# One order of start-up work for another in a fused tokenizer, attention and expert kernel: the gate's tanh, the token projection, the norm of pair 1 and the first maxima are moved

## The reference, cut to what matters

```python
def dwconv(x, wd, wp, bp):            # 3x3 depthwise, then 1x1
    return conv(conv(x, wd, pad=((1, 1), (1, 1)), groups=x.shape[1]), wp, bp)
loc  = dwconv(gelu(conv(x, pl_w, pl_b, stride=16)), pl_dw, pl_pw, pl_pwb)
g    = gelu(conv(wavelet_packet(x), pg_w1, pg_b1))
glob = conv(gelu(dwconv(g, pg_dw, pg_pw, pg_pwb)), pg_w2, pg_b2)
gate = 0.5 * (jnp.tanh(alpha) + 1.0)
h = (1.0 - gate) * loc + gate * glob
h = relu(dwconv(h, f1_...)); h = relu(dwconv(h, f2_...))
t = tokens(dwconv(loc + h, f3_...))
t = (t - mean(t)) / sqrt(var(t) + 1e-05) * ln_g + ln_b
h = concat([cls, t, txt], axis=1)
h = h + attn(layernorm(h))            # 12 heads of 16, own key masked
h = h + ffn(layernorm(h))             # z-scored logits, softmax, then the best 2 of 4 experts
```

## Time and profile before

| | before |
|---|---|
| median of 3 runs | 1234.02 us (1228.44 to 1234.77) |
| the profiled execution | 1228.34 us, its span 1226.7 us |
| TensorE busy | 1097.7 us, 89% of the span |
| VectorE busy | 679.3 us, 55% |
| ScalarE busy | 394.5 us, 32% |
| mean granted TensorE clock | 0.947 |
| chain that ended last | TensorE 63%, VectorE 16%, ScalarE 4% of the span |

### The profile page before, as it was taken

One profiled execution on the slowest core, in us unless ns is written; L12 is line 12 of the kernel. 1 busy time (PEld: TensorE's weight loads), 2 busy tenths in 40 slices (PEclk: granted clock), 3 DMA queues, 4 the chain that ended last, 5 costly groups with the idle time before them and its releaser, 6 DMA issues.

```text
span 1226.7 us, 19327 instructions
## 1 busy us (share of the span) xinstructions
PE 1097.7 (89%) x7731; PEld 809.0 (66%) x7731; DVE 679.3 (55%) x1890; ACT 394.5 (32%) x901; POOL 45.5 (4%) x81
## 2 busy tenths in 40 slices
PE   4898797888799999899989998999899989888895
PEld 3443464555486678568857875777588657676795
DVE  1378666564744666557654765476547643623432
ACT  1222132223324333443334333432343234223221
POOL 4200000100000000000000000000000000000000
PEclk8999899999989899989999998999899999788998
DMA  9100061422052014203320332042204220040000
GB/s 262 50 1 0 20 176 29 74 60 38 16 116 46 9 40 101 46 9 59 82 46 9 71 69 45 10 87 53 46 9 87 53 46 2 10 87 2 2 9 9
DMA packets 39441, 60.80 MB, mean 50 GB/s; under 512 B 6660, under 2 KB 31224, under 8 KB 38776
## 3 DMA queue, kind: packets, MB, share of 16 engines
q1 hardware_dynamic: 36256, 56.84, 21.5%
q10 hardware_dynamic: 3096, 2.74, 0.9%
HBM read 42.77 MB, written 16.34 MB: 48 GB/s over the span
## 4 chain that ended last, share of the span: by engine, by line
PE 63%; DVE 16%; ACT 4%; issue 2%; DMA 1%; SPq 1%; POOL 0%; DVEq 0%; POOLq 0%
PE PS L696 15%; PE PS L674 12%; DVE mx L1368 7%; PE PS L795 6%; PE PS L889 5%; PE PS L830 5%; PE PS L803 4%; PE PS L836 3%; PE PS L898 2%; PE PS L845 1%; DMA qst<-mrows 1%; PE PS L927 1%; PE PS L770 1%; PE PS L1019 1%; DVE acc L724 1%
## 5 line engine op out<-in xcount | busy, mean ns | idle before, releaser
L696 PE MATMUL PS<-w,hid 128*128 128x192 f32 x1152 | 231.1, 339 | 2.5 <-DVE acc L724 1.9
L709 ACT ACTIVATE hid<-PS,b 128x370 f32<-128x370 f32 x192 | 109.2, 569 | 316.7 <-PE PS L674 315.1
L696 PEld LDWEIGHTS PS<-w,hid 128*128 128x128 f32 x1152 | 197.8, 197 | 13.2 <-issue 5.1
L1368 DVE TENSOR_REDUCE mx<-PS 128x2 f32<-128x356 f32 x288 | 127.4, 519 | 131.7 <-PE PS L830 99.0
L1107 ACT ACTIVATE probs<-PS 128x356 f32<-128x356 f32 x288 | 110.9, 486 | 22.3 <-PE PS L830 12.8
L674 PE MATMUL PS<-x2T_hi,w_hi 128*128 128x370 f32 x192 | 91.9, 479 | 0.0
L845 PE MATMUL PS<-masks,ident_bf 128*128 128x256 bf16 (+1 forms) x288 | 73.4, 256 | 0.0
L889 PE MATMUL PS<-probs,va 128*17 128x178 f32 x1536 | 67.3, 315 | 6.4 <-ACT probs L1107 6.4
L795 PE MATMUL PS<-xT,w_at 96*96 96x370 f32 x192 | 68.2, 500 | 2.6 <-ACT xT L1067 1.7
L830 PE MATMUL PS<-kst,qst 96*128 96x178 bf16 x384 | 64.7, 264 | 6.3 <-issue 2.2
L770 PE MATMUL PS<-masks,ident_bf 128*128 128x356 bf16 x351 | 62.4, 327 | 4.0 <-POOL hid L1693 4.0
(11 more groups left out here) (232 smaller groups left out, 1727.3 us busy)
## 6 DMA issues: line engine op xcount, KB each, us to landing
qst<-scr_q SPq DMA_DIRECT2D x96, 144.0 KB, 4.6
scr_q<-qs SPq DMA_DIRECT2D x16, 432.0 KB, 3.3
scr_k<-ks SPq DMA_DIRECT2D x16, 432.0 KB, 4.1
kst<-scr_k SPq DMA_DIRECT2D x16, 432.0 KB, 5.0
kst<-scr_k SPq DMA_DIRECT2D x16, 288.0 KB, 5.9
cols<-in_x_cols SPq DMA_DIRECT2D x6, 392.0 KB, 12.7
w<-in_w SPq DMA_DIRECT2D x1, 2304.0 KB, 29.4
kst<-scr_k SPq DMA_DIRECT2D x16, 144.0 KB, 6.3
```

The costliest lines, as they stand in the source:

```text
L696: ins = nc.tensor.matmul(tile_psum((6, 7), i), hid[u % 2][:, 128 * i:128 * i + 128], w2[:, u, :], start=(j == 0 and i != 1), stop=(j == FT ...
L709: nc.scalar.activation(hid[u % 2][:, 0:XN], PS[:, 4 + u % 2, 0:XN], ACT.Relu, bias=b1[:, u:u + 1]).then_inc(S["h_ready"], 1)
L1368: nc.vector.tensor_reduce(out, PS[:, g, 0:T2].rearrange("p (b j) -> p b j", b=2), AX.X, ALU.max)\
```

## The change

Ten edits, all ahead of the end of round one.

1. ScalarE copies the wavelet product into `cw` first and does the gate's tanh after it. The load of `rows` goes from ScalarE's queue to SyncE's, and a load `w_f3` of 147 KB is new.
2. In the first block TensorE has unread products at three more places: 7 ahead of the first 1x1 product, 5 and 9 ahead of those of step 2, 12 ahead of the last depthwise step.
3. The token projection is cut: images 0 to 6 in the first block, 7 to 15 at the start of the second. Its operands `flat`, `w_f3`, `mid` and `f3_bias` now lie in the space of `probs`, so that they live on.
4. The bias sum goes to the second block: first pair 0's tokens alone, the rest after the norm of pair 0's input.
5. `preset` is GpSimd's alone and is awaited at 1. VectorE's clearing goes behind the norm of pair 0's input and has a semaphore of its own, `cleared`, that the first maxima wait for.
6. The unread products in `pe_first` write bank 2 up to pair 1's turn; 44 become 40 and 85 become 70.
7. `tok_norm(dve, 1, PAIRS)` becomes `tok_norm(dve, 1, 2)`; the norm of pairs 2 to 7 goes into round one, behind the split of s = 1's query. GpSimd waits for it before it copies pair 2.
8. In round one the maxima of s = 0 are made in six units in PSUM banks 4 to 6, set between the steps of s = 1's front; they stood behind it.
9. `WARM` has fewer products in that front (31 become 16) and 4 for 15 behind it.
10. In round one `x2T_lo` is made between the query's split and the key's.

```diff
-    "norm": 4, "query": 9, "key": 6, "value": 0, "kc": 4, "g": 3, "u": 5, "ss": 4,
-    ("max", 0): (0, 0, 0, 0, 0, 0), ("split", 0): 15, ("rows", 0): 22, ...
+    "norm": 0, "query": 4, "key": 3, "value": 0, "kc": 3, "g": 2, "u": 4, "ss": 4,
+    ("max", 0): (0, 0, 0, 0, 0, 0), ("split", 0): 4, ("rows", 0): 22, ...
...
+        def tokens_of(lo, hi):
+            for i in range(lo, hi):
+                q, b = divmod(i, 2)
+                for k in range(2):
+                    ins = nc.tensor.matmul(PS[64 * b:64 * b + 64, 4 + q // 2, D * (q % 2):D * (q % 2) + D],
+                                           flat[:, k, NI * i:NI * i + 64], w_f3[:, k, :],
+                                           start=(k == 0), stop=(k == 1), skip_group_check=True)
+            ins.then_inc(f3_psum, 1)
...
-                    act.wait_ge(ld_const, 32)
-                    nc.scalar.activation(gate[:], chan[0:HC, C_ALPHA:C_ALPHA + 2], ACT.Tanh).then_inc(gate_ready, 1)
-
                     act.wait_ge(haar_psum, 1)
...
                     ins.then_inc(haar_ready, 1)
+
+                    act.wait_ge(ld_const, 32)
+                    nc.scalar.activation(gate[:], chan[0:HC, C_ALPHA:C_ALPHA + 2], ACT.Tanh).then_inc(gate_ready, 1)
...
+                    def warm(n):
+                        for _ in range(n):
+                            nc.tensor.matmul(PS[:, 7, 0:T2], ident_bf[:], masks[:], start=True, stop=True)
                     def depthwise(r, n, lo=PE_TAP0, hi=9):
+                        if r == 4 and n == 1:
+                            warm(12)
...
                         if r == 0:
                             pe.wait_ge(apart_ready, 2)
+                            pe.wait_ge(casts, 1)
+                            warm(0 if n else 7)
+                        if r == 2:
+                            warm(9 if n else 5)
...
+                    pe.wait_ge(flat_ready, 1)
+                    tokens_of(0, B // 2 - 1)
...
         def pe_first(pe):
-            pe_warm(44)
+            pe.wait_ge(flat_ready, 2)
+            tokens_of(B // 2 - 1, B)
+            pe_warm(40, 2)
             pe_turn_in(pe, 0, 0)
...
-            pe_warm(85)
+            pe_warm(70, 2)
...
+            pe.wait_ge(S["cleared"], 1)
...
         def dve_first(dve):
+            dve.wait_ge(f3_psum, 1)
+            nc.vector.tensor_tensor(img_tok[:, 0, :], ps[:, 0, 0], f3_bias[:, 0, :], ALU.add).then_inc(S["tok_sum"], 1)
+            dve.wait_ge(S["tok_sum"], 1)
             tok_norm(dve, 0, 1)
             splits = dve_front0(dve, 0)
+            nc.vector.memset(PS[:, 3, :], 0.0)
...
+            dve.wait_ge(f3_psum, 2)
...
             dve_value(dve, 0, 0)
-            tok_norm(dve, 1, PAIRS)
+            dve.wait_ge(S["tok_sum"], 2)
+            tok_norm(dve, 1, 2)
...
+                def unit(u):
+                    if beside:
+                        pe_max_unit(pe, 0, a, u, 4)
                 pe_turn_in(pe, 1, b)
+                if beside:
+                    pe_stacked(pe, 0, a)
+                    pe.wait_ge(S["v_ready", 0], at(a, 1, 1))
+                unit(0)
...
                 pe_query(pe, 1, b)
+                unit(1)
...
                 pe_key(pe, 1, b)
+                unit(2)
...
             last.finish()
+            for u in units[0:3]:
+                dve_max_unit(dve, 0, a, u, 4)
...
+            if m is None and a is not None:
+                tok_norm(dve, 2, PAIRS)
...
-                splits(b)
+                splits(b, low if m is None else None)
```

More of the change, by code:

```diff
@@ L114 @@
 WARM = {
-    "norm": 4, "query": 9, "key": 6, "value": 0, "kc": 4, "g": 3, "u": 5, "ss": 4,
-    ("max", 0): (0, 0, 0, 0, 0, 0), ("split", 0): 15, ("rows", 0): 22, ("exp", 0): (0, 0, 0, 0, 0, 0), ("out", 0): 0,
+    "norm": 0, "query": 4, "key": 3, "value": 0, "kc": 3, "g": 2, "u": 4, "ss": 4,
+    ("max", 0): (0, 0, 0, 0, 0, 0), ("split", 0): 4, ("rows", 0): 22, ("exp", 0): (0, 0, 0, 0, 0, 0), ("out", 0): 0,
     ("max", 1): (2, 2, 2, 2, 2, 0), ("split", 1): 15, ("turn", 0): 6, ("back", 0): 4, ("rows", 1): 4,
@@ L819, in pe_value, with pe_logits @@
             pe_tokens(front(s, r), 4 * s + 2, xT[s], S["v_psum", s])
-        def pe_logits(pe, s, r, u, rows_, still, move, read, filled):
+        def pe_logits(pe, s, r, u, rows_, still, move, read, filled, first=0):
             for bank in range(3):
@@ L918, in pe_deviation @@
             ins.then_inc(S["kc_psum"], 1)
+            unit(3)
             moe.point("kc")
@@ L928, in pe_deviation @@
             ins.then_inc(S["g_psum"], 1)
+            unit(4)
             moe.point("g")
@@ L935, in pe_deviation @@
             ins.then_inc(S["u_psum"], 1)
+            unit(5)
             moe.point("u")
@@ L1264, in dve_front0, with splits @@
             dve_scaled(0, h_in(r), xn[0]).then_inc(S["xn_ready", 0], 1)
-            def splits(before):
+            def splits(before, between=None):
                 dve.wait_ge(S["q_f32", 0], at(r, 1, 1))
@@ L1271, in splits @@
                 dve.wait_ge(S["q_split", 0], at(r, 1, 1))
+                if between is not None:
+                    between()
                 dve.wait_ge(S["k_f32", 0], at(r, 1, 1))
@@ L1337, in dve_front1 @@
             moe.point("kc")
+            for u in units[3:4]:
+                dve_max_unit(dve, 0, a, u, 4)
             dve.wait_ge(S["g_psum"], at(r, 1, 1))
@@ L1343, in dve_front1 @@
             ins.then_inc(S["g_ready"], 1)
+            for u in units[4:5]:
+                dve_max_unit(dve, 0, a, u, 4)
             moe.point("g")
@@ L1437, in dve_round @@
             if b is not None:
-                query = dve_front1(dve, b, a, moe, last)
+                query = dve_front1(dve, b, a, moe, last, tuple(range(HH)) if m is None else ())
                 if a is None:
@@ L1483, in dve_round @@
                 moe.point("next query")
-                splits(b)
+                splits(b, low if m is None else None)
             moe.rest()
-            if b is not None:
-                dve.wait_ge(S["x2T_ready"], at(b, 1, 1))
-                nc.vector.tensor_tensor(x2T_lo[:], PS[:, 2:4, 0:XW], x2T_hi[:], ALU.subtract).then_inc(S["x2T_lo"], 1)
+            if b is not None and m is not None:
+                low()
             if nxt is not None:
```

124 lines of the change are left out of this document (68 added, 56 removed).

## The result

The changed kernel takes 1193.45 us (median of 4 runs, 1191.27 to 1193.72) where the kernel before takes 1231.23 (4 runs, 1228.42 to 1234.77). The ratio is 0.9688, 95% interval 0.9653 to 0.9723. The prediction was 1197 with a range of 1188 to 1210. In the profiled executions the span went from 1226.7 to 1191.9 us, 34.8 less, where my sum was 35.0. That the two agree so well is in good part luck, as the ledger shows: two terms were too large, one leg lost, and the last rounds, which were to give nothing, made up for it.

The account below looks back on a forecast made before the run. In start-up and round one no engine is full and the order of steps counts. The terms sum to 35.0 us, giving 1193.3 against the profiled execution or 1199.0 against the median; forecast 1197, range 1188 to 1210.

Parts of the forecast that it names:

- the prediction's own signs: Marks to check; wrong if the convolution stalls, eight depthwise products again take 4 us, or later rounds change length.
- item 2: First block's depthwise steps: unread products fill TensorE's stands and take back nearly all VectorE's waits, 3.6 us.
- Rival C: Round one doesn't hide the work: ScalarE's chain or VectorE's nine microseconds land on the path; 24.8 left, 1208; chance 0.12.
- 1, the tanh: Start of first block: with the copy ahead of the tanh, the big convolution starts near 13.5 and gains 10.7 us.
- Moving `rows` to SyncE's queue ... nothing: Start-up loads: `rows` then stands behind `cols` and ahead of weights needed 100 us later, so worth nothing.
- 3 and 4, the meeting and the start of block two: Between blocks: first block ends at ScalarE's `flat` copy, gaining 6.2 us; TensorE's longer start to pair 0's turn costs 1.9.
- 5, pair 1's norm: Second block's start-up: norming pair 1 alone brings its turn earlier and removes a half-clock stretch, 7.2 us.
- 6, maxima in the front's gaps: Round one: maxima hidden in the front's gaps bring ScalarE's row copy to 26.35 instead of 32.55, 6.2 us.
- 7, the norm in round one: Round one: norm of pairs 2 to 7 is hidden in VectorE's wait with 2.7 us to spare, cost 0.
- rival B: The clock falls in the new places too: gain 27.8 us, time 1204 to 1206; chance 0.17.
- 8, `x2T_lo`: Round one: made ahead of the key's split, it lets the gate products start earlier, 3.0 us.
- The later rounds: Rounds behind the edits: nothing edited, TensorE busy nearly throughout, so an earlier shift reaches the end whole; own gain 0.

Follow-up runs that it names:

- t1: Kernel before with only the copy into `cw` put ahead of the gate's tanh, loads unchanged; median 1230.51 us of 10 runs, ratio 0.9967.
- t3: Kernel before with only the load of `rows` moved from ScalarE's queue to SyncE's, the tanh still first; 1237.12 us, one run.
- t2: Kernel before with both the copy ahead of the tanh and `rows` on SyncE's queue; median 1222.71 us of 9 runs, ratio 0.9919.
- b0: The kernel before run again with no edit, for its spread; 1229.01 us, span 1227.4.
- c2: Changed kernel with 20 unread products instead of 40 ahead of pair 0's turn; median 1191.63 us of 4 runs.
- w0: Changed kernel without the 7, 5, 9 and 12 unread products of the first block; median 1198.99 us of 4 runs, ratio 0.9738.
- a0: The changed kernel run again with no edit, for its spread; median 1191.5 us of 6 runs.
- u7: Changed kernel with the norm of pairs 1 to 7 back in one piece in the start-up; median 1199.38 us of 4 runs, ratio 0.975.
- u6: Changed kernel with round one's maxima behind the front again and the old `WARM` table; median 1199.07 us of 4 runs, ratio 0.9774.
- u10: Changed kernel with the low part of `x2T` back behind the key's split in round one; 1189.76 us, one run.

## Why the prediction was right, point by point

The total is right; the sum behind it is less so. By the prediction's own signs two things went wrong: eight products again took 5.54 us in the depthwise steps, and the later rounds were not as long as before. Two marks were missed with them: the second block starts at 130.96 and not near 127.5, for the most part because item 2 gave 0.4 for 3.6, and a wait of VectorE for the taps of 2.22 us stayed at the first step where none above 0.3 was to be left. Rival C's arithmetic is off by 1.0 as well: 35.0 less 4.2, 4 and 3.0 leaves 23.8 and not 24.8.

**1, the tanh (10.7): right in size, wrong in cause.** The gain is 10.7 and 11.0. But the step "Moving `rows` to SyncE's queue ... nothing" failed, and with it the reading that ScalarE's issues end at 11.05 whatever the order. In t1's profile the order alone gains nothing; t3 shows the load alone to gain 3.0 to 4.6, t2 both together nearly all. The table load at 11.05 in the earlier trace rows came from an execution in which the issues ended early; in b0 and t1 they ended at 21.1 and 20.2. Either of two waits holds the copy back, `ident` in the one and the issues in the other, and both have to go. The start itself, 13.41 for 13.5, is luck: my 12.33 was the end of a table load that ended at 11.02, and what held the copy was the wavelet products, which took 6.46 us for 5.60. In two of the nine profiles, c2 and w0, it is the load that ends last.

**2, unread products in the depthwise steps (3.6): mis-sized, 0.4 here and 2.7 in a0.** The step that failed is that the clock is held wherever a stand is filled. The seven at the first step fill 1.2 us and leave stands of 1.50 and 0.47 around them, and the 1x1 group ran at half clock in three profiles of eight, at full clock in four.

**3 and 4, the meeting and the start of block two (6.2 and -1.9): right in the first pair**, 4.5 for 4.3. The meeting comes 6.2 after the flat copy before and at once after it now, and the turn 13.19 after the meeting for 11.48: 6.2 and -1.7. It is 3.0 in the second pair, as b0 took 16.15 for this leg where the first profile took 17.65. c2 bears out that the 40 products stand in the way by 2.9.

**5, pair 1's norm (7.2): right**, 7.3 (8.2 in the second pair), and u7 puts the same 7.3 back.

**6, maxima in the front's gaps (6.2): a little low.** 7.0 in both pairs: the front was lengthened 0.8 less than I had walked through (25.59 for my 26.35).

**7, the norm in round one (0): right by itself, but the leg behind the hidden maxima lost 0.5 to 4.8.** VectorE's spare was 4.24 for my 2.7. What I had put at nothing was TensorE's clock behind the rearranged first half of the round; by u6 and u7 that loss belongs to item 6 (with its `WARM` table), whose net worth is so 2.2 in the first pair and 5.4 in the second. This is rival B, in a place that I had not named.

**8, `x2T_lo` (3.0): right in kind**, 3.4 by u10 against a0, less against the others; 1.0 net of round two in the first pair of profiles (2.2 less 1.2).

**The later rounds (0): wrong by 8.3 in the compared profiles.** The step that failed is that a shift gained ahead of them reaches the end whole because nothing in them is edited. The last leg took 165.8 instead of 174.1. Over five profiles with before's rounds (before, b0, t1, t2, t3) this last leg took 168.7 to 174.1, mean 171.1; over nine with after's 165.8 to 171.1, mean 167.7. By this leg alone 3.4 would go with the change. But the legs ahead of it scatter too, and not by themselves: from the high part of `x2T` in round two to the end of the span, all of it without an edit, the five took 765.7 to 776.4, mean 769.8, and the nine 759.9 to 765.9, mean 762.5. So about 7 us go with the change on average. The medians say the same: they differ by 37.8, and by about 39 between the kernel before (1230.92) and a0, where the edited part gave 27.2 and 34.4. The windows of this leg, before:

```profile
1052.00:1082.00 30.00, 24.41 (x104) 19.02 (x102) 17.81 (x55) 6.58 (x16) 1.48 (x2) 0.70 0.18 42
1082.00:1112.00 30.00, 25.89 (x137) 21.85 (x137) 9.88 (x18) 8.18 (x13) 0.00 (x0) 0.85 0.30 57
1112.00:1142.00 30.00, 26.95 (x256) 21.18 (x254) 8.10 (x23) 12.47 (x33) 0.00 (x0) 0.94 0.01 2
```

and after:

```profile
1026.00:1056.00 30.00, 23.93 (x104) 17.72 (x104) 17.52 (x55) 6.40 (x16) 1.33 (x2) 0.75 0.24 54
1056.00:1086.00 30.00, 27.54 (x177) 24.29 (x176) 14.10 (x29) 9.30 (x15) 0.00 (x0) 0.96 0.24 45
1086.00:1116.00 30.00, 26.90 (x257) 21.83 (x256) 6.90 (x25) 13.44 (x34) 0.00 (x0) 1.00 0.01 2
```

The work is the same and the clock is higher. Why the shifted start meets better clock in the last rounds stays open; no run separates it. This gain made up what item 2 fell short by (3.2) and what the leg behind the hidden maxima lost (4.8), and so the sum came out at 34.8.

## What to carry to other kernels

Look at the duration of an engine's load issues, not only at its waits: an engine that issues many loads at the start can be held in the issuing itself, in one execution and not in the next, and where it is, neither its order nor the awaited tile matters. Here one large load moved to another queue ended it in all eleven profiles that have the move. When two waits hold one instruction, undo each alone before pricing either. And price what is hidden in a gap together with the stand that it leaves behind: price the clock as a range per stretch, and compare marks in two or more profiles of each kernel, since two profiles of one program here differ by up to 3.2 us in a stretch.

## What the runs showed of the hardware that was not expected

- Issuing a 12 KB load took 0.65 to 1.63 us in the eleven profiles with `rows` in another queue. With its 768 KB ahead in the same one it took 1.65 us in one execution of the kernel before, 8.94 in another (b0) and 9.15 in t1.
- The same instructions, with the same stands ahead, ran eight products in 5.54 us in one execution of the changed kernel and in 2.87 in another (half and full clock). Where the slow stretch falls differs between executions, and these eight products cost 2.7 us more or less by that alone.
- The kernel before ranged from 1221.47 to 1235.24 us over ten runs of one job, 1.1%, and an eleventh took 1241.13. The last leg ranged by 5.4 us over the five profiles with its rounds. Both are more than most items of this change.
